# Sharing the one-hot rows of two expert routers out among VectorE, ScalarE and GpSimd

## The reference, cut to what matters

```
# first: 8 experts, 2 per token
logits = einsum('bsd,de->bse', x, Wr) + br ;  top_idx = top_k(logits, 2)
weights = softmax(where(mask, logits, -1e9))
out += (relu(x @ W1[e] + b1[e]) @ W2[e] + b2[e]) * weights[e]        # for each expert e
# second: 32 experts, 4 per token
scores = sigmoid(x @ gate_w.T) ;  topk_ids = top_k(scores + e_bias, 4)
out = sum over the 4 experts of (silu(x @ w1[e]) * (x @ w3[e])) @ w2[e] * weight
```

## Time and profile before

| | |
|---|---|
| runs of the kernel | 1303.31, 1304.46, 1308.37 us; median 1304.46 us |
| profiled execution, its own time | 1302.33 us |
| its span | 1300.2 us, 24083 instructions |
| PE matmul, busy | 1149.5 us (88%), 7131 instructions |
| VectorE (DVE) | 727.2 us (56%), 1961 instructions |
| ScalarE (ACT) | 591.1 us (45%), 1438 instructions |
| GpSimd (POOL) | 336.9 us (26%), 540 instructions |
| mean granted TensorE clock | 0.933 of full speed |

### The profile page before, as it was taken

How to read it: one execution, slowest core, us unless ns; L and a number is a source line. 1 busy time by engine, 2 the same in 40 slices (tenths; PEclk the granted TensorE clock), 3 DMA queues, 4 the chain that set the end, 5 groups by cost and what they waited for, 6 DMA issues and landing times. The chain is left out here.

```text
span 1300.2 us, 24083 instructions
## 1 busy us (share of the span) xinstructions
PE 1149.5 (88%) x7131; PEld 761.3 (59%) x7132; DVE 727.2 (56%) x1961; ACT 591.1 (45%) x1438; POOL 336.9 (26%) x540
## 2 busy tenths in 40 slices
PE   4859999999997899999999999988666999974777
PEld 2749999999984423333333333325546899974666
DVE  6652222222238678888888888823673655531337
ACT  2632222121235437777777777776362333321233
POOL 2012222222212571110201111010015554346440
PEclk9959999999999969999999999999758999986979
DMA  5476667666763540412304304054126999985663
GB/s 154 157 274 205 235 220 232 220 231 222 225 198 82 165 57 2 52 22 31 52 2 52 43 10 52 2 122 98 42 69 180 279 283 290 256 230 154 206 186 119
DMA packets 145917, 185.59 MB, mean 143 GB/s; under 512 B 18278, under 2 KB 120416, under 8 KB 145690
## 3 DMA queue, kind: packets, MB, share of 16 engines
q1 hardware_dynamic: 134442, 153.30, 42.3%
q0 software_dynamic: 11376, 31.08, 8.3%
HBM read 141.29 MB, written 42.83 MB: 142 GB/s over the span
## 5 line engine op out<-in xcount | busy, mean ns | idle before, releaser
L2187 ACT ACTIVATE arena<-ps 128x512 f32<-128x512 f32 (+1 forms) x576 | 301.7, 598 | 119.6 <-PE ps L2095 118.8
L2216 DVE TENSOR_REDUCE arena<-ps 128x1 f32<-128x512 f32 x496 | 318.2, 682 | 60.0 <-PE ps L2054 56.6
L2095 PE MATMUL ps<-arena 99*128 99x512 bf16 (+1 forms) x576 | 216.1, 387 | 3.1 <-ACT arena L2187 2.7
L2054 PE MATMUL ps<-arena 96*128 96x512 bf16 x496 | 195.0, 395 | 5.5 <-DVE arena L2216 3.4
L1311 PE MATMUL ps<-scratch,arena 128*128 128x128 f32 x1140 | 154.4, 288 | 46.6 <-issue 24.7
L1311 PEld LDWEIGHTS ps<-scratch,arena 128*128 128x128 f32 x1140 | 143.6, 202 | 51.9 <-issue 32.4
L2095 PEld LDWEIGHTS ps<-arena 99*128 99x128 bf16 (+1 forms) x576 | 57.0, 101 | 173.8 <-ACT arena L2187 137.5
L2084 PE MATMUL ps<-arena 128*17 128x512 f32 (+1 forms) x1152 | 152.7, 602 | 2.1 <-ACT arena L2187 1.0
L1080 PEld LDWEIGHTS ps<-scratch,arena 128*128 128x128 f32 x1248 | 148.2, 195 | 3.7 <-issue 1.8
L1080 PE MATMUL ps<-scratch,arena 128*128 128x128 f32 x1248 | 148.7, 278 | 1.2 <-ACT scratch L1118 1.2
L1093 PE MATMUL ps<-arena,scratch 128*128 x624 | 141.0, 379 | 0.0
(11 more groups left out here) (340 smaller groups left out, 1357.7 us busy)
## 6 DMA issues: line engine op xcount, KB each, us to landing
arena<-in_L_ffn_W SPq DMA_DIRECT2D x47, 1024.0 KB, 10.2
arena<-in_L_ffn_w SPq DMA_DIRECT2D x190, 192.0 KB
y<-arena SPq DMA_DIRECT2D x38, 320.0 KB
y<-ysb SPq DMA_DIRECT2D x95, 128.0 KB
arena<-q_parts SPq DMA_DIRECT2D x96, 64.0 KB
arena<-k_parts SPq DMA_DIRECT2D x42, 137.6 KB
arena<-y SPq DMA_DIRECT2D x16, 256.0 KB, 6.9
arena<-in_L_ffn_w SPq DMA_DIRECT2D x8, 512.0 KB, 9.9
```

The lines of the kernel that those rows point to most:

```text
L2054: nc.tensor.matmul(ps[:, MAXB + pos % NMAXB, :], e.q_aug[u][0:QROWS, c, h, t * P:(t + 1) * P], e.k_aug[u][0:QROWS, h, CL + k * HB:CL + (k ...
L2095: nc.tensor.matmul(ps[0:rows, SB + n % NSB, :], e.k_aug[u][0:AROWS, h, k0:k0 + rows], e.q_aug[u][0:AROWS, c, h, :], start=True, stop=True) ...
L2187: nc.scalar.activation(e.prob[s % 2][0:rows, h, :], ps[0:rows, SB + (s * GH + h) % NSB, :], ACT.Exp).then_inc(p_ready, 1)
L2216: v.tensor_reduce(e.mx[:, c, h, t, k:k + 1], ps[:, MAXB + pos % NMAXB, :], AX.X, ALU.max).then_inc(max_done, 1)
```

## The change

GpSimd takes over some of the one-hot rows, with the same tensor_scalar as VectorE's. In the first router it makes row 3 of each turn; VectorE makes rows 1 and 2, ScalarE row 0 as before. In the second it makes rows 2 and 3 of each turn, VectorE row 1, and ScalarE row 0 in every turn: `WA` becomes (1, 1). That is 8 rows in the first router and 32 in the second for GpSimd, 8 and 24 fewer for VectorE, and 8 fewer (16 activations) for ScalarE in the second. PE waits for the new rows on a semaphore of their own, `pool_row`, and the counts of `col_ready` change accordingly. GpSimd waits for its tables (`pool_step`), for `parts_ready` and, from turn 2 on, for `pick_used`.

```diff
@@ first_router, gpsimd
         g_.memset(zero, 0.0).then_inc(zero_set, 1)
+        pool.wait_ge(pool_step, 1)
+        pool.wait_ge(parts_ready, 1)
+        pf, rf = flat(r.part), flat(r.row1)
+        for t in range(TURNS):
+            q = t * W + W - 1
+            if t >= 2:
+                pool.wait_ge(pick_used, q - 2 * W + 1)
+            g_.tensor_scalar(r.row_is[t % 2][:, W - 1, :], e.iota[:], pf[:, q:q + 1], rf[:, q:q + 1], ALU.is_equal, ALU.mult).then_inc(pool_row, 1)
@@ first_router, vector
-            for u in range(1, W):
+            for u in range(1, W - 1):
@@ first_router, tensor
             for u in range(W):
+                made = t * (W - 1) + 1
                 if u == 0:
                     pe.wait_ge(row_ready, t + 1)
-                    pe.wait_ge(col_ready, t * W + 1)
+                    pe.wait_ge(col_ready, made)
+                elif u == W - 1:
+                    pe.wait_ge(pool_row, t + 1)
                 else:
-                    pe.wait_ge(col_ready, t * W + 1 + u)
+                    pe.wait_ge(col_ready, made + u)
@@ second_router
-    N, W, WA = NTILE * E1, 4, (1, 2)
+    N, W, WA, WP = NTILE * E1, 4, (1, 1), 2
@@ second_router, gpsimd
+        pool.wait_ge(pool_step, 1)
+        pool.wait_ge(parts_ready, 1)
+        pf, rf = flat(r.part), flat(r.row1)
+        for t in range(TURNS):
+            for u in range(W - WP, W):
+                q = t * W + u
+                if t >= 2:
+                    pool.wait_ge(pick_used, q - 2 * W + 1)
+                g_.tensor_scalar(r.row_is[t % 2][:, u, :], e.iota[:], pf[:, q:q + 1], rf[:, q:q + 1], ALU.is_equal, ALU.mult).then_inc(pool_row, 1)
@@ second_router, vector
-            for u in range(WA[t % 2], W):
+            for u in range(WA[t % 2], W - WP):
@@ second_router, tensor
-                made = t * W - rows_before(t) + t
+                made = t * (W - WP) - rows_before(t) + t
                 if u < WA[t % 2]:
...
+                elif u >= W - WP:
+                    pe.wait_ge(pool_row, t * WP + u - (W - WP) + 1)
```

More of the change, by code:

```diff
@@ L702, in first_router @@
     off_ready, row_ready, col_ready, pick_used, token_raw = (sem("ro0_" + n) for n in ("off_ready", "row_ready", "col_ready", "pick_used", "token_raw"))
+    pool_row = sem("ro0_pool_row")
     first_ready, first_raw, expert_ready = (sem("ro0_" + n) for n in ("first", "first_raw", "expert_ready"))
@@ L858, in second_router @@
     off_ready, row_ready, col_ready, pick_used, token_raw = (sem("ro1_" + n) for n in ("off_ready", "row_ready", "col_ready", "pick_used", "token_raw"))
+    pool_row = sem("ro1_pool_row")
     first_ready, first_raw, token_ready, expert_ready = (sem("ro1_" + n) for n in ("first", "first_raw", "token_ready", "expert_ready"))
-    N, W, WA = NTILE * E1, 4, (1, 2)
+    N, W, WA, WP = NTILE * E1, 4, (1, 1), 2
     TURNS = NTILE * K1 // W
```

## The result

The changed kernel took 1313.9 us (median of 7 runs, 1310.5 to 1317.0) where the kernel before took 1303.3 us (7 runs, 1301.5 to 1308.4): ratio 1.008, 95% interval 1.0055 to 1.0106. So it is slower, by 10.4 us (7.2 to 13.8). The forecast was 1301.5 us with a range up to 1308.5. The profiled execution of the changed kernel took 1313.93 us.

The account below looks back on a forecast made before the run. VectorE was taken to set the second router's pace, at 1.105 us a turn. Second router -2.2 us and first -0.8 sum to -3.0, from the median 1304.46 to 1301.5 us; range 1296.5 to 1308.5.

Parts of the forecast that it names:

- the price of a GpSimd row: Both routers: one 128x128 compare-and-multiply row on GpSimd taken as 0.38 us, between 0.29 and 0.47.
- the high bound of 0.68: GpSimd row: 0.254 us plus 112 columns at 3.8 ns, as if each of two operations cost that slope.
- a meeting with a column tile: Second router: VectorE's tile holds GpSimd off for 0.39 us of streaming, less 0.2 of start-up, once a turn.
- VectorE's one-input rows exclude too: VectorE's rows, 0.07 us of streaming, use both read paths and so also hold GpSimd off.
- VectorE would lose half of a hold: First router: one GpSimd row beside VectorE costs VectorE perhaps 0.1 us a turn.
- Rival B: Second router: GpSimd becomes the bound, slower above 0.46 us a row; 1308.9 us at 0.6, 1311.9 at 0.68; chance 0.20.
- 2c + 0.19: Second router: GpSimd's chain per turn in us, with c the price of one GpSimd row.
- Rival C: Both routers: engines exclude each other for whole instructions; second router's turn 1.62 us, total 1315.3 us; chance 0.05.
- GpSimd runs one turn ahead of use by its two buffers: Added waits: PE waits for GpSimd's rows last in a turn, with GpSimd already one turn ahead.
- Behind it nothing hides this: After the second router: its gain of 2.2 us passes on; PE, SP and the expert stage only shift.
- Turn 0.84: First router: a turn falls to 0.84 us, near ScalarE's floor of 0.82; eight turns gain 1.3 us, less 0.1.
- my 0.8: First router: of 1.2 us gained, 0.8 passes on through gathers in full DMA engines.

Follow-up runs that it names:

- e8: Changed kernel, but GpSimd makes three rows a turn in the second router and VectorE none: ratio 1.0114 to the kernel before.
- e10: Changed kernel, but VectorE makes each column tile of the second router twice, once into an unread buffer: turn 1.95 us against 1.67.
- e4: Changed kernel, VectorE's second-router tile and row cut to 4 columns from turn 2 (not the reference's token list): GpSimd row 787 ns, turn 1.54 us.
- e11: Kernel before, without GpSimd rows, VectorE making one more unread column tile each turn of the second router: +8.9 us (+5.6 to +12.1).
- e12: Kernel before, without GpSimd rows, VectorE making three more unread column tiles each turn of the second router: +21.2 us (+17.2 to +25.3).
- e9: The changed kernel measured again, on the same chip as the three-row kernel: ratio 1.0080 (1.0054 to 1.0107), +10.4 us.
- e3: Changed kernel, but GpSimd makes one row a turn in the second router instead of two, VectorE two: 1301.42 us, ratio 0.9986.
- e7: Changed kernel, GpSimd's second-router rows 64 columns wide instead of 128 from turn 2 (not the reference's): turn 1.45 us against 1.67.

## Why the prediction was wrong

*The step that failed* is the price of a GpSimd row: "I take 0.38: this row has the one input of the cheap form but one operation more, so it lies between 0.29 and ... 0.47". It measured 0.77. It was mis-sized by two, and outside the high bound of 0.68 too. That bound's form is not far off: it had 3.8 ns a column, the half-width row shows 3.4; but its 0.254 us at 16 columns leave 0.19 us that don't depend on width, and this row has 0.33. The larger error was to lean to the low side. L327 is another operation, with a mask and no second operation, and "one input" said nothing about what each operation costs: the second, with its pointer scalar, is 0.19 us.

*Side by side.* I had charged 0.19 us for a meeting with a column tile, 0.39 of streaming less 0.2 of start-up. The turn shows 0.12, and e8 leaves only 0.03 of it to the tile; the second tile of e10 costs 0.28. So a meeting has no one price here, and no run separates the streaming from the start-up. That VectorE's one-input rows exclude too was borne out by e8, at about 0.09 us a row. That VectorE would lose half of a hold in the first router was wrong: its column tiles there keep their median of 0.306 us, and in the second router they grow by 0.02. The section "Who interferes with whom" of the Trainium skill's page "SBUF — State Buffer", read as blocking for the whole instruction, is not what these runs show: the tiles that start in the middle of a GpSimd row are at most 0.02 us longer for it, where 0.4 us of that row are still to go.

*The second router.* Rival B was the mechanism: GpSimd never idle, PE waiting for it 30 times, turn above 1.1. Its formula 2c + 0.19 gives 1.73 us with c = 0.77; the turn is 1.67. B stopped at c = 0.68 and 1311.9 us, a sum that leaves out the first router's -0.5 which its case at 0.6 has. Rival C's turn of 1.62 and 1315.3 us lie close to what was measured by accident: it took short rows and full exclusion, and e4 rules that out. "GpSimd runs one turn ahead of use by its two buffers" is true only of an engine that is faster than the loop. "Behind it nothing hides this" was right within the intervals, and e11 and e12 show it.

*The first router.* Turn 0.84 was nearly right (0.78 and 0.87 in the last two turns); the gain was 0.7 us, not 1.2, and one row of 1.74 us is part of the reason: in e9, where that row took 1.48, the gain was 0.9. 0.5 us of it arrived at PE, against my 0.8. Like the forecast's -3 us it is beneath what a total can tell.

*The chances.* I gave "slower by over 0.5%" 0.09, though B's break-even, c = 0.46, stood 0.08 us above my estimate of a row that no trace had shown. That distance, against an uncertainty of a factor of two, called for B at least as high as the forecast.

## What to carry to other kernels

Before work goes to another engine, write down the break-even price of the moved instruction (here 0.46 us) and ask what row of the trace shows that very form, with its operations, scalars and width. If none does, neighbours bound it poorly, and the estimate belongs to the side of the slower engine. And shares go by price: here GpSimd at 0.77 us a row can take one row of a turn of 1.0 us, not two.

## What the hardware did unexpectedly

A GpSimd tensor_scalar with two operations on 128x128 costs 0.77 us from start to start, 6.0 ns a column, three times VectorE's 0.26 us for the same row. The Trainium skill, page "GPSIMD Engine Reference", section "Engine selection", calls one-input work there roughly line-rate; for this form the trace disagrees. With immediates for both scalars the recorded instruction is 0.64 us long, but the rows still come 0.72 us apart: the length in the record is not the price.

What a GpSimd row lost to VectorE depended on where in the row they met: nothing when the column tile started 0.37 us into it, 0.03 us when the row started 0.15 us before the tile's end (e8), 0.41 when a whole tile and a VectorE row fell on it (e10), and about 2 us once in e3. What decides it isn't shown.

On the chip of e4 to e7 the kernel before took 1230.8 us against 1302 elsewhere. The windows show one place where such a chip is faster. Behind the second router, 1147 to 1207 us, the kernel before on the first chip, and e7 on the other:

```profile
1147.00:1207.00 60.00, 35.78 (x207) 31.50 (x206) 14.77 (x46) 9.84 (x34) 31.18 (x33) 0.74 0.63 182
```

```profile
1150.70:1210.70 60.00, 60.00 (x444) 56.23 (x443) 31.86 (x99) 29.97 (x105) 44.83 (x49) 1.00 0.96 308
```

PE is busy 36 of 60 us on one and all 60 on the other, with DMA at 182 and 308 GB/s. Since e7's token list is not the reference's, this shows the pauses' absence, not their cause, which no run here looked for.
